# Two short products of zeros in each slot of the last attention's heads

## The reference, cut to what matters

```
qh = (q @ Wq + bq) ...            # 16 heads of 8 columns
kh = (k @ Wk + bk) ...
vh = (v @ Wv + bv) ...
scores = jnp.einsum('bhqd,bhkd->bhqk', qh, kh) * scale
attn = jax.nn.softmax(scores, axis=-1)
out = jnp.einsum('bhqk,bhkd->bhqd', attn, vh)
return concat @ Wo + bo
```

## Time and profile before

| what | us |
|---|---|
| median of 3 runs | 802.28 |
| lowest, highest | 799.08, 804.95 |
| the profiled execution, its time | 800.18 |
| the profiled execution, its span | 798.4 |

### The profile page before, as it was taken

One profiled execution on the slowest core, in us unless ns is written; L12 is line 12 of the kernel. 1 busy time (PEld: TensorE's weight loads), 2 busy tenths in 40 slices (PEclk: granted clock), 3 DMA queues, 4 the chain that ended last, 5 costly groups with the idle time before them and its releaser, 6 DMA issues.

```text
span 798.4 us, 16192 instructions
## 1 busy us (share of the span) xinstructions
PE 718.4 (90%) x5744; PEld 532.7 (67%) x5744; DVE 493.9 (62%) x1309; ACT 412.4 (52%) x1047; POOL 290.0 (36%) x398
## 2 busy tenths in 40 slices
PE   6577899899898998999999989989898999999886
PEld 3355566675666666799898977857576455767665
DVE  3658996877968787344543456545455658684653
ACT  2124557666575676744544458655563544454311
POOL 0103564565645666310000018323431545454300
PEclk9979999999999999999999999999999656999999
DMA  7273552534627273000000000001011411000000
GB/s 242 73 187 82 122 126 68 132 70 95 136 55 204 60 202 127 1 1 1 1 1 1 1 1 4 1 1 36 6 41 50 153 63 28 5 2 9 8 7 7
DMA packets 25175, 48.10 MB, mean 60 GB/s; under 512 B 7265, under 2 KB 14193, under 8 KB 25097
## 3 DMA queue, kind: packets, MB, share of 16 engines
q1 hardware_dynamic: 24376, 45.66, 22.2%
q10 hardware_dynamic: 720, 1.41, 0.5%
HBM read 17.49 MB, written 0.52 MB: 23 GB/s over the span
## 4 chain that ended last, share of the span: by engine, by line
PE 63%; DVE 17%; issue 9%; ACT 7%; POOL 2%; DMA 1%; SPq 0%; POOLq 0%; DVEq 0%; ACTq 0%
PE G L523 8%; PE SC L778 7%; PE SC L765 7%; PE SC L708 5%; PE G L569 4%; PE SO L751 3%; DVE shift_cols L1478 3%; PE SC L800 3%; PE G L877 3%; ACT causal_probs L1092 2%; PE SC L684 2%; PE SO L832 2%; PE SM L725 2%; PE G L591 2%; PE G L528 2%
## 5 line engine op out<-in xcount | busy, mean ns | idle before, releaser
L1107 ACT ACTIVATE exps<-SC 128x512 f32<-128x512 f32 x192 | 114.1, 596 | 108.2 <-PE SC L708 107.7
L1478 DVE TENSOR_REDUCE shift_cols<-SC 128x2 f32<-128x512 f32 x192 | 129.8, 684 | 30.3 <-PE SC L684 29.5
L1557 POOL TENSOR_TENSOR rstd<-variance,consts 128x2 f32<-128x2 f32 (+1 forms) x48 | 37.2, 774 | 278.7 <-DVE variance L1171 275.6
L1626 POOL TENSOR_TENSOR VB<-exps 128x256 f32<-128x256 f32 x128 | 94.9, 749 | 63.1 <-ACT exps L1107 62.3
L1081 ACT ACTIVATE hidden<-SC,cols 128x256 f32<-128x256 f32 x128 | 53.5, 470 | 65.5 <-PE SC L765 65.3
L1648 POOL TENSOR_TENSOR causal_probs<-causal_probs,inverse 128x256 f32<-128x256 f32 x64 | 51.6, 827 | 68.9 <-DVE inverse L1491 68.9
L1512 DVE SCALAR_TENSOR_TENSOR R<-SC,small,R 128x128 f32<-128x128 f32 x128 | 39.0, 346 | 54.1 <-PE SC L778 53.5
L1092 ACT ACTIVATE causal_probs<-SC,negmax 128x128 f32<-128x128 f32 (+1 forms) x128 | 52.1, 423 | 37.2 <-DVE negmax L1486 37.0
L778 PEld LDWEIGHTS SC<-ffn_w,hidden 128*128 128x128 f32 x512 | 66.0, 192 | 5.3 <-issue 1.8
L708 PE MATMUL SC<-stacked_q,stacked_k 100*128 100x256 f32 x256 | 65.5, 338 | 3.2 <-DMA stacked_q<-shift_rows 1.6
L778 PE MATMUL SC<-ffn_w,hidden 128*128 128x128 f32 x512 | 67.6, 276 | 0.0
(11 more groups left out here) (244 smaller groups left out, 1497.7 us busy)
## 6 DMA issues: line engine op xcount, KB each, us to landing
stacked_k<-k_hi SPq DMA_DIRECT2D x64, 128.0 KB, 2.3
stacked_q<-q_hi SPq DMA_DIRECT2D x64, 128.0 KB, 2.3
ffn_w<-in_ffn_w SPq DMA_DIRECT2D x16, 512.0 KB, 4.5
stacked_k<-k_lo SPq DMA_DIRECT2D x32, 128.0 KB, 2.3
stacked_q<-q_lo SPq DMA_DIRECT2D x32, 128.0 KB, 2.3
packed_k<-U SPq DMA_DIRECT2D x48, 32.0 KB, 1.9
packed_q<-YN SPq DMA_DIRECT2D x48, 32.0 KB, 1.9
a_weights<-in_a_li SPq DMA_DIRECT2D x3, 256.0 KB, 7.8
```

What stands on the lines that cost most here:

```text
L1107: fn(exps[:, n % EXPS, :, :].rearrange("p t q -> p (t q)"), SC[1][:, n % 2, :, :].rearrange("p t q -> p (t q)"), ACT.Exp, scale=ATTENTIONS ...
L1478: v.tensor_reduce(shift_cols[:, n // UNIT % 4, :, n % UNIT], SC[0][:, n % 2, :, :], axis=AX.X, op=ALU.max, negate=True).then_inc(head_max, 1)
L1626: v.tensor_tensor(kept[n % EXPS].rearrange("p t q -> p (t q)"), exps[:, n % EXPS, 0, :], exps[:, n % EXPS, 1, :], ALU.add).then_inc(kept_r ...
```

## The change

A tile of zeros, 128 x 144, is made once by GpSimd. In the 41 slots from `LX_AT + 4` = 239 to `LX_AT + 44` = 279, TensorE does, in `front` behind `head_products` and ahead of `turn_shifts`, two fp32 products of that tile: 128 rows, 128 columns of weights, (128 + 16) / 4 = 36 moving columns. They are written to a tile of ring "g". The first product signals the tile filled, the second signals it emptied. Nobody reads it.

```diff
+OCCUPIED = (LX_AT + 4, LX_AT + 45)
...
+        zeros = sb("zeros", [P, C + HEADS])
...
+        ones_made, z_zeroed, zeros_made = sem("ones_made"), sem("z_zeroed"), sem("zeros_made")
...
+                def occupy(slot):
+
+                    key, half = ("zeros", slot), (C + HEADS) // 4
+                    g = fill(pe, "g", key)
+                    mm(g[:, 0:half], zeros[:, 0:C], zeros[:, 0:half], start=True, stop=True).then_inc(*filled(key))
+                    mm(g[:, 0:half], zeros[:, 0:C], zeros[:, 0:half], start=True, stop=True).then_inc(*emptied(key))
...
                 def front(slot):
                     if head_of(slot) is not None:
                         head_products(head_of(slot))
+                    if slot == OCCUPIED[0]:
+                        pe.wait_ge(zeros_made, 1)
+                    if OCCUPIED[0] <= slot < OCCUPIED[1]:
+                        occupy(slot)
                     if unit_of(slot, TURN_AT) is not None:
...
                 for b in range(NB):
                     v.memset(Z[b][0:BUCKET, 0, :], 0.0).then_inc(z_zeroed, 1)
+                v.memset(zeros[:, :], 0.0).then_inc(zeros_made, 1)
                 pool.wait_ge(consts_in, 16)
```

More of the change, by code:

```diff
@@ L390, in decoder @@
         dve_chain, pool_chain = sem("dve_chain"), sem("pool_chain")
-        ones_made, z_zeroed = sem("ones_made"), sem("z_zeroed")
+        ones_made, z_zeroed, zeros_made = sem("ones_made"), sem("z_zeroed"), sem("zeros_made")
         kv_drawn, q_exp, q_normal, context_ready = (per_batch_sem(n) for n in ("kv_drawn", "q_exp", "q_normal",
```

## The result

The changed kernel takes 843.9 us (median of 4 runs, 839.18 to 858.7) against 803.62 us for the kernel before in the same session: 1.0489 times as long, 95% interval 1.0414 to 1.0565. The forecast was 824.5 with a range to 838. The direction was right, the size was not. The profiled execution has a span of 837.4 us against 798.4, 39.0 more.

A forecast was written before the change was run, and what follows sets the result against it. TensorE, 90% busy and partly at half clock in the last attention, was taken as the bound. Terms of +1.8, +20.1 less 0.4, +3.8 and -1 gave +24.3 on the profiled 800.18 us: 824.5 us, range 792 to 838.

The forecast's parts named there:

- What bounds the stage: In the last attention's half-clock stretches TensorE is the bound, 17.10 of 17.1 us busy, so anything added there lies on the path.
- The price of a set: Two fp32 zero products in one slot, four load-and-pass pairs: 0.91 us at half clock, 0.49 at full.
- The two states that hold themselves: In the occupied slots, full clock with zeros stays full and half stays half; the entry decides, with the fall at 619.5.
- The 22 occupied slots of heads 12 to 33: Slots 12 to 33 at half clock: 22 x 0.91 = +20.1 us, less 0.4 us idle.
- the two lost full stretches: Two 3.4 us full-clock stretches among the heads fall to half: work takes 10.6 us in place of 6.8, +3.8.
- slots 34 to 44, clock back: ... -1: Last 11 occupied slots, clock returned: TensorE and VectorE 18.3 us each in a 20.5 us stretch, taken as -1.
- and then the zeros hold it: After the out-projection tiles of slots 267 and 268 the clock returns and zeros keep it at 1.0.
- rival B: Half clock up to slot 280, as zeros separate the out-projection tiles: +40.6, 841 us, chance 0.12.
- Slots 4 to 11: Eight occupied slots at full clock: 8 x 0.49 = 3.9 us, less 2.1 us of TensorE idle time, +1.8.
- The ring of two banks: Ring "g" at out-projection slots 240/241 and 267/268: waits for VectorE's drain, between nothing and 2 us, taken as nothing.
- Rival D: Zeros, loads included, count in full and the clock never falls in the occupied stretch: -8.5, 792 us, chance 0.17.

## Why the prediction was wrong in size

**What bounds the stage** held. TensorE was the bound in the half stretches, and what was added there lay on the path in full.

**The price of a set** held: 0.88 and 0.47 us measured, 0.91 and 0.49 forecast. The rows of neighbouring shapes (8, 64 and 128 columns) bounded it well. The rule of the Trainium skill (TensorE: Matmul & The Clock Gate, section LDWEIGHTS), columns over 1.2, which is 107 ns for 128 columns, would by my estimate have given 0.43 us a set. That is near the 0.47 at full clock and half of the 0.88 at half clock. Nor does its rule that the clock follows how busy the engine has been (same page, "What's actually happening") agree: TensorE was busy in all of the 64.9 us at half.

**The two states that hold themselves** held for the first part. The clock fell at the entry in spite of eight sets ahead of it, the zeros kept it at half, and it came back only behind the out-projection tiles. The 22 occupied slots of heads 12 to 33, up to the start of head 34, lost 22.5 us; the sum had 23.5 (20.1 - 0.4 + 3.8). This hides errors that cancel. By the kernel without the sets of heads 14, 18, ..., 30 a set costs 0.9 us here, 19.8 for 22. In two slots, those of heads 16 and 24, it also cuts apart scores that had run side by side, 0.8 us each. I had written that the zeros push the scores apart and put no price on it. Together that is 21.4 us, and by this estimate about 1 us is left for the two lost full stretches, where the sum had 3.8. No run separates that term alone.

**The step that failed** is the last term of the sum, "slots 34 to 44, clock back: ... -1". The clock did come back, but "and then the zeros hold it" was wrong: 6.8 us later it fell and stayed at half for 23.9 us. From head 34 to head 45 the term measured +9.7 (26.1 us against 16.4), and +10.4 with the slot of head 33. The kernel with zeros in the last 12 slots alone shows the same 10.4 us. In the earlier trace rows the clock falls 6.8 us after it has come back at the same tiles. The forecast's ground for a hold was that zeros fill idle time at the full clock. They did, TensorE is busy in 6.80 of those 6.8 us against 6.04 before, and the clock fell all the same. With the sets of heads 36, 40 and 44 left out the clock stays, with all twelve it doesn't. Leaving out three others (heads 34, 38 and 42, with those of the earlier units) did not help. Each of these is read from one profiled execution. The times of all runs agree with it: the kernel without the three takes 830.14 us, as much as the one with no set in the tail (831.14), and each of its four runs is below each of the changed kernel. The mechanism stays open, since the one set among the three that runs before the clock falls cuts no scores apart. I had listed the half clock in the tail as rival B at 0.12 and 841 us, for another reason (the zeros separating the out-projection tiles; that did not keep the clock from returning). The profiled execution, 839.2 us, lies between the forecast and B, close to B, but with 3.9 us that arose before the zeros and a return of the clock that B denies: that closeness is partly luck.

**Slots 4 to 11**: +1.8 forecast, +2.7 measured. The idle time was filled as forecast, 0.06 us is left of 2.1. But the clock fell at 624.6, 1.8 us before head 12 starts (626.4), where in the kernel before the two were 0.3 us apart. Half of 1.8 us is the missing 0.9, an estimate.

**Chance**: 3.9 of the 39.0 us of the profiled execution arose before the first set. The forecast left room for that only in its range. The median of the four runs, 843.9 us, is a further 4.7 above the profiled execution, and no trace shows where that lies.

**The ring of two banks** was taken as nothing. At half clock it is: TensorE is the late engine and no such wait shows in the changed kernel. At full clock it is 3.5 us in one place, at a tile that the forecast did not name (the query and key tile of slot 263, not the out-projection tiles). Whoever mends the clock meets this wait next.

**Rival D** is out for these products: the clock fell at the entry. With 144 columns it doesn't fall, but the loads are the same in both kernels, so the loads don't count as D has it, and even then the stage gains nothing over before.

## What to carry to other kernels

With the same loads, filler products of 36 columns left the clock at half and those of 144 columns kept it at 1.0, for 0.59 us a set in place of 0.47 at full clock. So price filler by its time, loads included, and read its effect on the clock from a trace rather than from how busy the engine is. Look first at whether the engine is already full at the low clock: there filler only adds its own time. And look at what runs side by side on different row groups before a product of all rows is put between.

## What the runs showed that I had not expected

- Products of 32 rows on four different row groups start within 0.02 us of each other (652.36 to 652.38), and a full-height set between two heads that ran so costs 0.8 us at half clock beside its own 0.88. In heads 12 to 33 that was so at two of the six sets tried.
- Three sets of 0.47 us each, out of twelve, decide whether the clock holds: 20.4 against 31.1 us for the same twelve heads. Only one of them runs before the clock falls.
- Holding the full clock with filler brought the stage nothing: heads 12 to 33 take 37.5 us at 1.0 with 12.4 us of filler, 36.8 at mostly 0.5 without any.
- Stretches of half clock fall at places that have nothing to do with an edit (at 604.2 for 3.4 us in the changed kernel, near the end in others: from head 63 to the end it took 79.6 us in some executions, 84.8 in others and 86.4 in one). Why they are there in one execution and not in another stays open.
